# Matrix normalisations of the last stage: eight batches on VectorE before, six on VectorE in PSUM and two on GpSimd after

## The reference, cut to what matters

```
H_res = sinkhorn_log(H_res_logits)          # one 4x4 matrix per token, tau 0.1, 50 iterations
# one iteration, written for the exponentials: divide each row by its sum,
# then divide each column by its sum; 50 times over
H_res = (1.0 - g) * I + g * H_res
x_pre = einsum('btnc,btn->btc', x_streams, H_pre)
y = x_pre @ W_branch
x_mixed = einsum('btij,btjc->btic', H_res, x_streams)
y_distributed = einsum('btc,btn->btnc', y, H_post)
return x_mixed + y_distributed              # times tanh(gate), added to x
```

## Time and profile before

| What | us |
|---|---|
| median of 3 runs | 2596.14 (2595.49 to 2597.87) |
| the profiled execution, its own time | 2597.39 |
| its span, first to last instruction | 2595.6 |
| first GpSimd instruction of `mix_streams` | 2404.43 |
| start of the first of the 99 calls on VectorE | 2438.30 |
| start of the first instruction after them | 2549.92 |
| first instruction that needs the finished matrices | 2551.35 |
| busy over the span: TensorE, VectorE, ScalarE, GpSimd | 2386.6, 1493.9, 1078.5, 1048.7 |

### The profile page before, as it was taken

How to read it: one execution, slowest core, us unless ns; L and a number is a source line. 1 busy time by engine, 2 the same in 40 slices (tenths; PEclk the granted TensorE clock), 3 DMA queues, 4 the chain that set the end, 5 groups by cost and what they waited for, 6 DMA issues and landing times. The chain is left out here.

```text
span 2595.6 us, 34684 instructions
## 1 busy us (share of the span) xinstructions
PE 2386.6 (92%) x12976; PEld 2201.3 (85%) x12976; DVE 1493.9 (58%) x2344; ACT 1078.5 (42%) x2448; POOL 1048.7 (40%) x844
## 2 busy tenths in 40 slices
PE   8999999979998899999889889999999999999714
PEld 6888888868998789999779779999999999999713
DVE  6222222123300567678667467888777777777797
ACT  3222222122311456667611155555555555554413
POOL 3000000000000356677554367777676766764110
PEclk9999999989999799999989999999999999999757
DMA  6222222143323222332133223333333333322001
GB/s 201 69 67 74 69 73 70 49 157 113 95 66 99 92 74 81 94 93 73 54 109 95 87 72 92 107 99 100 101 97 110 98 101 103 97 85 83 6 0 51
DMA packets 161241, 224.36 MB, mean 86 GB/s; under 512 B 31718, under 2 KB 124290, under 8 KB 160050
## 3 DMA queue, kind: packets, MB, share of 16 engines
q1 hardware_dynamic: 161074, 222.14, 27.7%
HBM read 183.81 MB, written 38.29 MB: 86 GB/s over the span
## 5 line engine op out<-in xcount | busy, mean ns | idle before, releaser
L1270 DVE TENSOR_TENSOR attend_w_lo<-attend_w_raw,attend_w_hi 128x1024 fp32r<-128x1024 f32 (+1 forms) x184 | 273.3, 1485 | 208.4 <-ACT attend_w_hi L1125 125.0
L1005 POOL TENSOR_TENSOR attend_w_hi<-attend_w_raw,attend_one 128x1024 fp32r<-128x1024 f32 (+1 forms) x178 | 332.7, 1869 | 126.6 <-DMA attend_w_raw<-in_wo 61.2
L1445 PE MATMUL attend_ps_gemm<-normed_hi,attend_w_hi 128*128 128x400 f32 x704 | 246.4, 350 | 21.8 <-DVE attend_w_lo L1270 21.8
L1141 ACT ACTIVATE attend_p<-attend_p,attend_neg_max 100x361 f32<-100x361 f32 x256 | 150.9, 591 | 260.7 <-DVE attend_neg_max L1309 260.7
L1445 PE MATMUL attend_ps_gemm<-attend_o_hi,attend_w_hi 128*128 128x400 f32 x704 | 250.6, 356 | 6.1 <-issue 4.4
L1445 PE MATMUL attend_ps_gemm<-normed_lo,attend_w_hi 128*128 128x400 f32 x704 | 244.9, 348 | 0.0
L1445 PE MATMUL attend_ps_gemm<-attend_o_hi,attend_w_lo 128*128 128x400 f32 x704 | 243.7, 346 | 0.0
L1445 PE MATMUL attend_ps_gemm<-normed_hi,attend_w_lo 128*128 128x400 f32 x704 | 243.6, 346 | 0.0
L1445 PE MATMUL attend_ps_gemm<-attend_o_lo,attend_w_hi 128*128 128x400 f32 x704 | 243.6, 346 | 0.0
L301 DVE TENSOR_TENSOR context_k_square<-context_k_rows 128x512 f32<-128x512 f32 (+1 forms) x46 | 31.8, 692 | 346.5 <-ACT context_k_rows L226 346.4
L1150 ACT ACTIVATE attend_p<-attend_p,attend_exp_inv 100x361 f32<-100x361 f32 (+1 forms) x384 | 207.8, 620 | 0.0
(11 more groups left out here) (302 smaller groups left out, 6405.6 us busy)
## 6 DMA issues: line engine op xcount, KB each, us to landing
attend_w_raw<-in_wq SPq DMA_DIRECT2D x88, 512.0 KB, 4.3
attend_w_raw<-in_wo SPq DMA_DIRECT2D x64, 512.0 KB, 4.3
middle_w_raw<-in_wf SPq DMA_DIRECT2D x26, 512.0 KB, 4.2
attend_w_raw<-in_wo SPq DMA_DIRECT2D x32, 384.0 KB, 3.8
context_ctx_raw<-in_ctxT SPq DMA_DIRECT2D x8, 1456.0 KB, 7.0
attend_k_raw<-scratch_k SPq DMA_DIRECT2D x64, 180.5 KB, 3.7
context_ctx_raw<-in_ctxF SPq DMA_DIRECT2D x22, 512.0 KB
scratch_v<-context_v_out SPq DMA_DIRECT2D x44, 256.0 KB, 2.1
```

The source lines that it names most:

```text
L1005: pool.tensor_tensor(hi, w_flat(w_raw, j % RAW, j), one[:hi.shape[0]].to_broadcast(hi.shape), ALU.mult).then_inc(w_hi_done, 1)
L1141: act.activation(p[:, slot, h], p[:, slot, h], ACT.Exp, bias=neg_max[:, slot, h:h + 1], accum_out=exp_sum[:, slot, h:h + 1]).then_inc(expe ...
L1270: dve.tensor_tensor(w_flat(w_lo, j % SPLIT, j), w_flat(w_raw, j % RAW, j), w_flat(w_hi, j % SPLIT, j).bitcast(F32), ALU.subtract).then_inc ...
L1445: mm = pe.matmul(out, left[a](c), right[b](c), start=(c == 0 and a == b == 0), stop=(c == chunks - 1 and a == 1))
```

## The change

One constant, `BD = 6`, divides the batches. The matrices of batches 0 to 5 (96 numbers per partition) are written by VectorE into the free part of the PSUM bank `ps_logits`, and its 99 calls of `normalise` work there: the sums go to PSUM too, the reciprocals to SBUF. The matrices of batches 6 and 7 (32 numbers per partition) stay in `h` in SBUF, and GpSimd does their 99 normalisations. Its `normalise` is four instructions, each waiting for the one before: the two halves of each row (or column) added, the two results added, the sums raised to the power of minus one, and the product. After every third normalisation one of the 32 additions of a part follows, where before these ran as soon as the parts came. VectorE scales its own six batches, waits for all 396 instructions of GpSimd, and scales the other two.

```diff
+    BD = 6
+        own_pair = sb("own_pair", [S, (B - BD) * N * 2])
+        own_sum = sb("own_sum", [S, B - BD, N])
+        minus_one = sb("minus_one", [S, B - BD])
         # gpsimd
-            for b in range(B):
-                for i in range(N):
-                    n = b * N + i
-                    pool.wait_ge(part_done, n + 1)
-                    pool.tensor_tensor(x[:, b, i * C:(i + 1) * C], x[:, b, i * C:(i + 1) * C], part[:, n % 4], ALU.add
-                                       ).then_inc(out_added, 1)
+            def step(ins):
+                count[0] += 1
+                ins.then_inc(own_chain, 1)
+                pool.wait_ge(own_chain, count[0])
+            own = h[:, BD:B]
+            pairs_j = own_pair[:].rearrange("p (b i j) -> p b i j", i=N, j=2)
+            pairs_i = own_pair[:].rearrange("p (b i j) -> p b i j", i=2, j=N)
+            def normalise(turn):
+                if turn:
+                    step(pool.tensor_tensor(pairs_i, own[:, :, 0:2], own[:, :, 2:4], ALU.add))
+                    step(pool.tensor_tensor(own_sum[:], pairs_i[:, :, 0], pairs_i[:, :, 1], ALU.add))
+                    sums = own_sum[:].unsqueeze(2).to_broadcast([S, B - BD, N, N])
+                else:
+                    step(pool.tensor_tensor(pairs_j, own[:, :, :, 0:2], own[:, :, :, 2:4], ALU.add))
+                    step(pool.tensor_tensor(own_sum[:], pairs_j[:, :, :, 0], pairs_j[:, :, :, 1], ALU.add))
+                    sums = own_sum[:].unsqueeze(3).to_broadcast([S, B - BD, N, N])
+                step(pool.tensor_tensor(own_sum[:], own_sum[:], minus_one[:].unsqueeze(2).to_broadcast([S, B - BD, N]), ALU.pow))
+                step(pool.tensor_tensor(own, own, sums, ALU.mult))
+            def add_part(n):
+                b, i = n // N, n % N
+                pool.wait_ge(part_done, n + 1)
+                pool.tensor_tensor(x[:, b, i * C:(i + 1) * C], x[:, b, i * C:(i + 1) * C], part[:, n % 4], ALU.add
+                                   ).then_inc(out_added, 1)
+            pool.memset(minus_one[:], -1.0).then_inc(consts, 1)
+            pool.wait_ge(consts, 7 + N)
+            pool.wait_ge(h_started, 1)
+            for k in range(2 * ITERS - 1):
+                normalise(k % 2 == 0)
+                if k % 3 == 2 and k // 3 < B * N:
+                    add_part(k // 3)
         # vector
+            hp = ps_logits[:S, 256:256 + BD * N * N].rearrange("p (b i j) -> p b i j", i=N, j=N)
+            side_p = ps_logits[:S, 384:384 + BD * N].rearrange("p (b n) -> p b n", n=N)
-            step(dve.tensor_tensor(h[:], h[:], rows(side2[:]), ALU.mult))
+            dve.tensor_tensor(h[:, BD:B], h[:, BD:B], rows(side2[:])[:, BD:B], ALU.mult).then_inc(h_started, 1)
+            step(dve.tensor_tensor(hp, h[:, 0:BD], rows(side2[:])[:, 0:BD], ALU.mult))
             def normalise(turn):
-                view = turned(h[:]) if turn else h[:]
-                step(dve.tensor_reduce(side[:], view, AX.X, ALU.add))
-                step(dve.reciprocal(side2[:], side[:]))
-                step(dve.tensor_tensor(h[:], h[:], (columns if turn else rows)(side2[:]), ALU.mult))
+                view = turned(hp) if turn else hp
+                step(dve.tensor_reduce(side_p, view, AX.X, ALU.add))
+                step(dve.reciprocal(side2[:, 0:BD], side_p))
+                step(dve.tensor_tensor(hp, hp, (columns if turn else rows)(side2[:])[:, 0:BD], ALU.mult))
-            step(dve.tensor_scalar(h[:], h[:], gates[:, 3:4], gates[:, 0:1], ALU.mult, ALU.mult))
+            step(dve.tensor_scalar(h[:, 0:BD], hp, gates[:, 3:4], gates[:, 0:1], ALU.mult, ALU.mult))
+            dve.wait_ge(own_chain, 4 * (2 * ITERS - 1))
+            step(dve.tensor_scalar(h[:, BD:B], h[:, BD:B], gates[:, 3:4], gates[:, 0:1], ALU.mult, ALU.mult))
```

More of the change, by code:

```diff
@@ L2133, in mix_streams @@
         out_added = sem("out_added")
+        h_started = sem("h_started")
+        own_chain = sem("own_chain")
         h_ready = sem("h_ready")
@@ L2170, in _ @@
             pool.memset(mean_w[:], 1.0 / D).then_inc(consts, 1)
-            for b in range(B):
-                for i in range(N):
-                    n = b * N + i
-                    pool.wait_ge(part_done, n + 1)
-                    pool.tensor_tensor(x[:, b, i * C:(i + 1) * C], x[:, b, i * C:(i + 1) * C], part[:, n % 4], ALU.add
-                                       ).then_inc(out_added, 1)
+            count = [0]
+            def step(ins):
[28 more added lines that the diff above has]
+                    add_part(k // 3)
         @block.tensor
```

## The result

| | before | after |
|---|---|---|
| median of 4 runs, us | 2595.81 | 2767.82 (2765.14 to 2769.96) |
| ratio | | 1.066, 95% interval 1.0647 to 1.0672 |
| span of the profiled execution | 2595.6 | 2768.1 |
| matrices finished | 2551.32 | 2723.86 |
| from there to the end of the span | 44.3 | 44.2 |

The direction was forecast, the size was not: 2638 was given, with a range up to 2700. Everything lies ahead of the finished matrices, as the last row says.

What follows compares the result with a forecast made beforehand. GpSimd's dependent chain was to bound the finished matrices: 2447.0 + 23.4 (additions) + 121.6 (96 normalisations) = 2592.0, plus 1.2 is 2593.2, 41.9 us later; 2597.39 + 41.9 = 2639.3, as median 2638. Range 2600 to 2700, own range 2608 to 2670.

Steps and rivals of the forecast that it cites:

- What bounds: Last stage: the change is worth only what it does to the moment the matrices are finished, 2551.32 us before, 41.9 later.
- GpSimd's simple instructions: GpSimd's normalisation: first addition 216 ns, second 198, product 251, together 665, with four gaps of 78 ns.
- The ratio of 1.96: Skill's GpSimd slowdown for two-input elementwise work: c would be 1684 ns, time 2678 us; counted within the dear case.
- The power: GpSimd's power on 8 numbers, in no row: 290 ns taken, floor 198 ns, above 0.8 us; normalisation 1267 ns.
- Dear power: Rival: GpSimd's power is its own routine, 0.8 us, time 2687; with dearer instructions, above 2670: 0.23, above 2700: 0.10.
- The additions: 32 additions of parts in the same GpSimd chain: 730 ns each, 23.4 us.
- The wait before the first addition: GpSimd, after three normalisations, stands for 6 us until the first part is there, with the matrices queued behind.
- VectorE's loop: 99 calls on six batches in PSUM: 94.6 us, ending at 2533.1, ahead of GpSimd's chain.
- The column sum: VectorE's column sum over 96 numbers: 320 ns against the row sum's 252, so column calls 989 ns, row calls 921.
- The tail: After the finished matrices: 44 us in either kernel, same slow TensorE beginning; 0, or 1.5 us less if warm.

## Why the prediction was wrong

- What bounds: right. The moment at which the matrices are finished carries the whole difference, and the tail is 44.2 against 44.3 us.
- GpSimd's simple instructions: right. 216, 198 and 251 ns were worked out from one row of 16 numbers and a line; 215, 202 and 240 came. The gaps are 79 ns for 78. The ratio of 1.96 that the Trainium skill, "GPSIMD Engine Reference", § 3, gives for large ones would, by estimate from VectorE's 166 to 192 ns, have made them 0.33 to 0.38 us; here they are 0.20 to 0.24.
- The power: this is the step that failed. It read "above, four times that, 0.8 us", and "I take 290 ns". It took 1.645 us. 96 x (1.645 - 0.290) = 130.1 us, and 2638 + 130 = 2768. Neither price came from a row of a power. For the 290 I carried the ratio of VectorE's reciprocal (6.3 ns per number) to its product, six, over to GpSimd, where a number costs 158 ns, some seventy times a product's 2.2; the upper end was four times the floor, with nothing behind the four. "Dear power" had the right mechanism and half the price; it left only 0.10 above 2700.
- The other terms cancel nearly. The additions took 0.68 us from start to start instead of 0.73 (-1.6), the three other instructions 9 ns less per call (-0.9), and this execution was 3.0 us later at the product that releases GpSimd's chain, 2.4 of them already at the stage's first GpSimd instruction (+2.9 at the first addition, which waited for its part). 2593.2 + 130.1 - 1.6 - 0.9 + 2.9 is 2723.7; 2723.86 was measured.
- The wait before the first addition was 2.0 us instead of 6: the three calls ahead of it had taken longer.
- VectorE's loop: right. 94.6 us were given and 2441.38 to 2534.60 is 93.2. The column sum in PSUM is as cheap as the row sum, which I had not taken.
- The tail: right, 44.2 against 44.3 us, so TensorE did not come to it warm. From 2438 us on the branch now runs at a granted clock of 0.50, its level of 1.2 GHz, where before it had 0.71 up to 2486, and the tail's first 64 products of TensorE take 16.2 us, against 16.3 before.

## What to carry to other kernels

A chain of small simple instructions, each waiting for the one before, costs its count times a fixed price and little else, so giving a quarter of the numbers to a slower engine gives it all of the count. Even with a free power the split lost 0.2%, as long as the 32 additions stood in the same queue. Cutting the count on the engine that has the chain (three instructions to two in 90 calls, at the price of an approximation) gained 1.3% on top of PSUM's 0.3%. And where an operation that is in no row is multiplied by a hundred, its price can decide alone: look at it in an idle corner of the kernel before building on it, and until then leave its upper end open.

## What the runs showed of the hardware that was not expected

- A power on GpSimd costs 0.37 us and 158 ns per number of a partition, with the two exponents tried (-1 and 0.5) alike. For its length it does not hold up a VectorE product with both inputs in SBUF: 0.26 us within a power of 1.65.
- On VectorE a column sum over numbers 4 apart cost 377 ns in SBUF and 299 in PSUM for 128 numbers, where the row sum cost 285 and 299. PSUM for input and output adds some 8 ns to a product and 14 to a row sum.
- The Trainium skill, "VectorE: DVE Perf Modes", the section on the TRN2 errata, has 62 cycles more of fixed cost from PSUM. These runs don't agree: a reciprocal of 32 from PSUM took 357 ns and from SBUF 353.
